# Second attention of a four-layer kernel: heads in slots of four, scores on four row groups, part of the softmax shift on GpSimd

## The reference, cut to what matters

```python
q = (x @ wq.T)...; k = (x @ wk.T)...; v = (x @ wv.T)...      # 32 heads of 8
scores = einsum('bhqd,bhkd->bhqk', q, k) / sqrt(8) + rel_bias
ctx = einsum('bhqk,bhkd->bhqd', softmax(scores), v)
x3 = layernorm(x2 + ctx @ wo.T)
```

## Time and profile before

| | |
|---|---|
| median of 3 runs | 955.1 us |
| profiled execution, its own time | 953.87 us |
| its span, first to last instruction | 951.8 us |
| mean granted TensorE clock | 0.978 |
| second attention, eight iterations | about 364 to 735 us, some 46.3 us each |
| busy TensorE, VectorE, ScalarE, GpSimd in one iteration | 44.7, 40.4, 44.0, 6.8 us |

### The profile page before, as it was taken

One profiled execution on the slowest core, in us unless ns is written; L12 is line 12 of the kernel. 1 busy time (PEld: TensorE's weight loads), 2 busy tenths in 40 slices (PEclk: granted clock), 3 DMA queues, 4 the chain that ended last, 5 costly groups with the idle time before them and its releaser, 6 DMA issues.

```text
span 951.8 us, 20997 instructions
## 1 busy us (share of the span) xinstructions
PE 866.0 (91%) x7200; PEld 711.0 (75%) x7200; DVE 702.3 (74%) x2130; ACT 687.0 (72%) x1538; POOL 261.3 (27%) x360
## 2 busy tenths in 40 slices
PE   3777899999999998999999999999998998999994
PEld 2556778788888887676777776767666987899994
DVE  6888878878875557888888989898987462365447
ACT  2778857768676337999999999999998322366646
POOL 0345542322343120200202021111112256334432
PEclk8889999999999999999999999999999999999998
DMA  6203021110010012010202020202021212244534
GB/s 200 67 1 98 15 79 62 40 35 13 13 45 13 24 34 61 21 28 1 70 2 70 1 70 2 69 1 59 10 66 48 86 62 94 73 109 124 133 136 174
DMA packets 54760, 54.85 MB, mean 58 GB/s; under 512 B 17953, under 2 KB 48929, under 8 KB 54658
## 3 DMA queue, kind: packets, MB, share of 16 engines
q1 hardware_dynamic: 51250, 44.18, 16.0%
q0 software_dynamic: 3408, 9.34, 2.8%
HBM read 32.85 MB, written 20.65 MB: 56 GB/s over the span
## 4 chain that ended last, share of the span: by engine, by line
PE 50%; DVE 19%; ACT 18%; issue 8%; DMA 2%; POOL 1%; another core or an unknown queue 1%; DVEq 0%; ACTq 0%; SPq 0%; POOLq 0%
PE ps L445 11%; PE ps L447 9%; PE ps L446 9%; PE ps L969 5%; ACT G L1492 4%; ACT G L1502 4%; ACT wu_rows L1492 3%; PE ps L986 3%; PE ps L957 2%; PE ps L677 2%; PE ps L692 2%; DVE G L2037 2%; ACT RT L1252 1%; PE ps L750 1%; DVE wu_rows L2037 1%
## 5 line engine op out<-in xcount | busy, mean ns | idle before, releaser
L1492 ACT ACTIVATE G<-G,small 128x256 f32<-128x256 f32 x296 | 133.7, 517 | 7.0 <-DVE small L2037 7.0
L445 PE MATMUL ps<-WU 128*128 128x256 f32 x384 | 117.4, 306 | 17.3 <-DVE wu_rows L1859 6.7
L2037 DVE CUSTOM_DVE_ANT_0 G<-ps,nb 128x256 f32<-128x256 f32 x296 | 111.6, 419 | 20.7 <-PE ps L957 17.8
L1502 ACT COPY G<-ps 128x512 f32<-128x512 f32 x192 | 113.3, 590 | 9.6 <-PE ps L969 9.5
L2398 POOL TENSOR_SCALAR_AFFINE_SELECT G<-G 128x256 f32<-128x256 f32 x128 | 76.3, 619 | 145.8 <-ACT G L1337 145.6
L446 PE MATMUL ps<-WU 128*128 128x256 f32 x384 | 108.7, 283 | 0.0
L447 PE MATMUL ps<-WU 128*128 128x256 f32 x384 | 108.6, 283 | 0.0
L1492 ACT ACTIVATE wu_rows<-wu_rows,small 128x256 f32<-128x256 f32 x216 | 98.1, 518 | 3.2 <-DVE small L2037 3.2
L969 PE MATMUL ps<-ident,G 128*128 128x128 f32 x592 | 92.6, 283 | 4.6 <-ACT G L1502 3.3
L2037 DVE CUSTOM_DVE_ANT_0 wu_rows<-ps,nb 128x256 f32<-128x256 f32 x216 | 81.6, 419 | 14.6 <-PE ps L957 13.4
L445 PEld LDWEIGHTS ps<-WU 128*128 128x128 f32 x384 | 73.1, 190 | 25.8 <-DVE WU L1865 9.5
(11 more groups left out here) (251 smaller groups left out, 2354.5 us busy)
## 6 DMA issues: line engine op xcount, KB each, us to landing
xs<-G SPq DMA_DIRECT2D x8, 645.0 KB, 6.5
G<-xs SPq DMA_DIRECT2D x39, 128.0 KB
G<-x SPq DMA_DIRECT2D x17, 256.0 KB, 3.4
G<-in_x SPq DMA_DIRECT2D x16, 256.0 KB, 2.8
wu_rows<-yy SPq DMA_DIRECT2D x8, 512.0 KB, 7.6
x<-G SPq DMA_DIRECT2D x15, 256.0 KB, 2.4
wu_rows<-in_wu SPq DMA_DIRECT2D x8, 384.0 KB, 5.7
wraw<-in_wu SPq DMA_DIRECT2D x8, 256.0 KB, 2.9
```

The source lines that it names most:

```text
L445: pe.matmul(o, lh, rh, start=start, stop=False, skip_group_check=True)
L1492: m = act.activation(p, p, ACT.Exp, scale=-1.0, bias=mneg[:, k:k + 1])
L1502: act.copy(probT(h), halves(2 + h % 2)).then_inc(probT_act, 1)
L2037: m = dve.tensor_tensor_reduce(prob(H2 * i + h)[:, t, :], ps[:, SCORE_BANKS[(H2 * i + h) % 3], S * t:S * (t + 1)], nbv[:, t, :], 1.0, -FMI ...
```

## The change

Heads are done in slots of four (`QUADS`, eight per iteration). `scores(i, q)` issues four heads into four banks, `SCORE_BANKS = (0, 1, 5, 6)`, and waits until all four heads of the slot before have been read. Turns of a quad are in the slot after; a mix covers eight heads, in slots 1, 3, 5 and 7, between scores and turns. Bank 6 is no longer there for the neighbours' work: it goes to bank 4, shared with the mixes (`SHARED_BANK`), and bank 7 (`DENSE_BANK`). For 12 heads of 32 the exponential moves behind the transpose: GpSimd subtracts the minimum in `prob`, TensorE turns the result, and ScalarE takes it with an exponential of 128x512 out of PSUM instead of a copy. ScalarE takes all heads. GpSimd's weight splits are laid between its subtractions.

```diff
+QUADS = H2 // 4
+SCORE_BANKS = (0, 1, 5, 6)
+SHARED_BANK, DENSE_BANK = 4, 7
+POOL_SHIFTS = (1, 2, 2, 1, 2, 1, 2, 1)
@@ banks of the neighbours' work
+        def b_qk(f, b, t):
...
+                return (DENSE_BANK if t else SHARED_BANK) if b else 6
@@ TensorE, scores
+                    if i or q:
+                        pe.wait_ge(biased_ready, 4 * (QUADS * i + q))
...
                     for t in range(2):
+                        for j in range(4):
                             r = slice(32 * j, 32 * j + 32)
+                            m = pe.matmul(ps[:, SCORE_BANKS[j], S * t:S * (t + 1)], QT[r, q, P * t:P * (t + 1)], KTT[r, q, :],
                                           start=True, stop=True, tile_position=(32 * j, 0))
+                    m.then_inc(score_ready[2], 1)
@@ TensorE, turn
+                    if j < POOL_SHIFTS[quad % QUADS]:
+                        pe.wait_ge(prob_shifted, shifts(n))
+                    else:
+                        pe.wait_ge(prob_ready, n + 1 - shifts(n))
+                    if n >= 2:
+                        pe.wait_ge(probT_taken, n - 1)
@@ TensorE, one iteration
+                    for q in range(QUADS):
+                        scores(i, q)
+                        if q == 1 and not first:
+                            pe.wait_ge(heads_k[2], 4 * i + 3)
+                            mix(i - 1, 3)
+                        if q == 3:
+                            if left:
+                                pe.wait_ge(v_staged[2], i + 2)
+                            mix(i, 0)
+                        if q == 5:
+                            if left:
+                                pe.wait_ge(split_hi[2], 8 * (i + 1) + 4)
+                                pe.wait_ge(split_ready[2], 4 * (i + 1) + 2)
+                            pe.wait_ge(o_copied[2], 4 * i + 1)
+                            mix(i, 1)
+                        if q == 7:
...
+                            mix(i, 2)
+                        before = H2 * i + 4 * q - 4
+                        if before >= 0:
+                            turn(before)
+                            turn(before + 1)
...
+                        if q == 5 and left:
...
+                            qk(2, i + 1, 1)
+                        if q == 6 and left:
+                            pe.wait_ge(split_ready[2], 4 * (i + 1) + 4)
+                            turned(QS, DENSE_BANK, 0)
+                            pe.wait_ge(o_copied[2], 4 * i + 2)
+                            turned(KS, SHARED_BANK, 0)
...
+                        if before >= 0:
+                            turn(before + 2)
+                            turn(before + 3)
+                        if q == 0 and left:
+                            heads_out(2, i, 2)
+                            pe.wait_ge(heads_q[2], 4 * i + 3)
+                            x_turn(2, i + 1)
...
+                        if q == 4 and left:
...
+                            qk(2, i + 1, 0)
@@ ScalarE
+                    if n % 4 < POOL_SHIFTS[n // 4 % QUADS]:
+                        act.activation(probT(n), halves(2 + n % 2), ACT.Exp, scale=-1.0).then_inc(probT_taken, 1)
+                    else:
+                        act.copy(probT(n), halves(2 + n % 2)).then_inc(probT_taken, 1)
...
+                    for q in range(QUADS):
+                        before = H2 * i + 4 * q - 4
+                        if before >= 0:
+                            take(before)
+                            take(before + 1)
...
+                        if before >= 0:
+                            take(before + 2)
+                            take(before + 3)
+                        if q == 4 and not first:
+                            context_hi(2, i - 1)
...
+                        for j in range(POOL_SHIFTS[q], 4):
+                            exponential(H2 * i + 4 * q + j)
+                        if q in (4, 5) and left:
+                            hi_parts(i + 1, q - 4)
@@ VectorE: least of the four heads first, take gone, then
+                        if q == 4:
+                            if not first:
+                                context_lo(2, i - 1)
+                            if left:
+                                qk_lo_parts(i + 1, 0)
+                        if q == 5:
+                            outputs(i, 1, first)
+                            if left:
+                                qk_lo_parts(i + 1, 1)
@@ GpSimd
+            def shifted(n):
+                pool.wait_ge(biased_ready, n + 1)
+                for t in range(2):
+                    k = 2 * (n % 8) + t
+                    p = prob(n)[:, t, :]
+                    m = pool.tensor_scalar(p, p, mneg[:, k:k + 1], None, ALU.subtract)
+                m.then_inc(prob_shifted, 1)
...
+                for q in range(QUADS):
+                    if q == 7 and i:
+                        layernorm_rstd(2, i - 1, 2)
+                    for j in range(POOL_SHIFTS[q]):
+                        shifted(H2 * i + 4 * q + j)
+                    if q == 0 and i < iterations[2] - 1:
+                        expert_part(i, 0)
+                    if q == 3:
+                        shared_part(i)
+                    if q == 5 and i < iterations[2] - 1:
+                        expert_part(i, 1)
```

More of the change, by code:

```diff
@@ L406, in raw_count, with shifts @@
             return 16 * sum(dmas(n) for n in range(load + 1))
[L408 to L422, removed]
+        def shifts(n):
+            quad, j = divmod(n, 4)
+            return (sum(POOL_SHIFTS) * (quad // QUADS) + sum(POOL_SHIFTS[:quad % QUADS])
+                    + min(j + 1, POOL_SHIFTS[quad % QUADS]))
         blk = ctx.enter_context(nc.Block())
@@ L668, in heads @@
             def heads(f, b, n):
-                for src, bank, out in ((QS, B_QT[f], heads_q[f]), (KS, B_KT[f], heads_k[f])):
+                for src, bank, out in ((QS, B_QT[f], heads_q[f]), (KS, b_kt(b, n) if f == 2 else B_KT0, heads_k[f])):
                     w = src.bitcast(F32).rearrange("p (t g c) -> p t g c", t=2, g=8)
@@ L944, in phase2, with turned @@
                 n = iterations[2]
[L946 to L952, removed]
+                def turned(src, bank, group):
+                    w = src.bitcast(F32).rearrange("p (t g c) -> p t g c", t=2, g=8)
+                    for g in range(2):
+                        for t in range(2):
+                            m = pe.transpose(ps[:, bank, S * g + P * t:S * g + P * (t + 1)], w[:, t, 2 * group + g, :], ident[:])
+                    m.then_inc(heads_turned[2], 1)
@@ L976, in mix @@
                         pe.wait_ge(vp_ready[2], i + 1)
[L977 to L988, removed]
+                    pe.wait_ge(probT_taken, H2 * i + 8 * g + 8)
@@ new lines, in mix @@
+                    for quad in (2 * g, 2 * g + 1):
+                        for kt in range(2):
+                            for j in range(4):
+                                h = 4 * quad + j
+                                at = (D2 + 1) * h
+                                m = pe.matmul(ps[32 * j:32 * j + 32, SHARED_BANK, S * (quad % 2):S * (quad % 2 + 1)],
+                                              vp[:, kt, at:at + 32], probT(h)[:, kt, :], start=kt == 0, stop=kt == 1,
+                                              skip_group_check=True, tile_position=(0, 32 * j))
@@ new lines, in one @@
+                        if q == 1:
+                            pe.wait_ge(heads_q[2], 4 * i + 4)
+                            turned(KS, DENSE_BANK, 3)
+                        if q == 2 and not first:
+                            c_turn(2, i - 1, 1, 8)
+                        if q == 3 and not first:
+                            c_turn(2, i - 1, 3, 8)
+                        if q == 4 and left:
+                            pe.wait_ge(heads_q[2], 4 * i + 4)
+                            pe.wait_ge(heads_k[2], 4 * i + 4)
+                            pe.wait_ge(o_copied[2], 4 * i + 1)
+                            qk(2, i + 1, 0)
@@ L1031, in phase2 @@
+                        if q == 6 and not first:
+                            if left:
+                                pe.wait_ge(heads_q[2], 4 * (i + 1) + 1)
+                            project(2, i - 1)
+                        if q == 7 and left:
+                            pe.wait_ge(heads_q[2], 4 * (i + 1) + 2)
+                            turned(KS, DENSE_BANK, 1)
                 passes(n, one)
                 pe.wait_ge(out_step[2], OUT_STEPS[2] * (n - 2) + 5)
+                pe.wait_ge(biased_ready, H2 * n)
@@ L1038, in phase2 @@
                     m.then_inc(xt_turned[3], 1)
-                for h in range(H2 - TURN_LAG, H2):
-                    turn(n - 1, h, False)
-                    if h == H2 - 3:
-                        mix(n - 1, H2 // 4 - 2, False)
-                mix(n - 1, H2 // 4 - 1, False)
+                for h in range(H2 - 4, H2):
+                    turn(H2 * (n - 1) + h)
+                pe.wait_ge(o_copied[2], 4 * n - 1)
```

(6 more changed lines are left out.)

271 lines of the change are left out of this document (136 added, 135 removed).

## The result

The changed kernel takes 1064.8 us (median of 4 runs, 1057.4 to 1066.0) against 955.3 before, a ratio of 1.114 with a 95% interval of 1.111 to 1.117. It is slower, as forecast, but by 109 us where I had said 48, and outside the range of 935 to 1040. The profiled execution took 1065.39 us, with a span of 1063.6.

The account below looks back on a forecast made before the run. TensorE and ScalarE were taken as nearly full. Work of 37.8 plus waits of 3.8, 4.5, 2.9 and 4.2 gave 53.2 us against 46.3, 6.9 more in seven iterations: 1003 us, range 935 to 1040.

Parts of the forecast that it names:

- waits that come: Step pricing TensorE's new waits per iteration from handoffs and fixed engine orders: 15.4 us counted.
- the three places: TensorE's waits at slot 5's mix, slot 6's first turned q and slot 2's turns: 11.2 us per iteration.
- The first rival: Waits are covered and the busiest engine, ScalarE, sets the period: 919 us, chance 0.17.
- Slot 5: The mix there waits for high and low parts standing behind a take and exponentials: 3.8 us per iteration.
- Slot 6: The first turned q there waits for its low parts after q and k product part 1: 4.5 us.
- The ring: Turns wait for takes standing behind exponentials, in slots 0, 1, 3, 4 and 7: together 4.2 us per iteration.
- Slot 2: Turns of heads GpSimd shifted wait, since GpSimd stands in a weight split awaiting its load: 2.9 us.
- the cast's slope: Price of GpSimd's 128x256 subtraction, taken from casts of 384 and 704 columns: 0.40 us each.
- TensorE's clock falls as well: Rival: idle in slots 5 and 6 brings half clock, 24 us more, 1027 us; chance 0.22.
- TensorE's own work: TensorE's work per iteration without waits, falling from 43.3 to 37.8 us.
- ScalarE's 38.6: ScalarE's work per iteration after the change, down from 43.0 us.
- the 0.60 for such a take: ScalarE's price in us for each of 12 takes with an exponential, set between 0.47 and 0.81.

Follow-up runs that it names:

- e6: Changed kernel with high parts of q and k early and GpSimd subtracting for no head: 984.8 us.
- e3: Changed kernel with GpSimd's expert splits in later slots, high parts earlier, and the first half of the q and k product earlier: 942.4 us.
- e4: Changed kernel with idle TensorE time filled by 34 products of 512 columns per iteration, in slots 2, 5 and 6: 1029.7 us.

## Why the prediction was wrong

**The direction and its reason were right.** The step "waits that come" named the three places, and all three are where TensorE waits. The first rival, that the busiest engine sets the period, describes e6 (984.8), and about a third of its gain of 36 us became real once the orders were mended (e3, 10 us under the kernel before).

One iteration of the kernel after, 61.5 us, can be taken apart by the marks of idle time in TensorE's timeline: they sum to 14.8 us. In e3, which issues the same work at full clock throughout, they sum to 3.7 of 44.0 us, so TensorE's work takes 40.3 us. The rest, 61.5 - 14.8 - 40.3 = 6.4 us, is my estimate of what half clock costs. The forecast had 15.4 of waits, 37.8 of work and 0 for the clock.

**The waits: right in sum, by luck.** Slot 5: 3.8 forecast, 3.55 in the trace. Slot 6: 4.5 forecast, 0.50 + 3.47. The ring: 4.2 forecast; the trace has 1.07 in slot 4 where I had 1.75, and 0.34 and 0.64 elsewhere, 2.05 in all. Slot 2: 2.9 forecast, 4.55 + 0.69 = 5.2 in the trace. The last two errors, of 2.2 and 2.3 us, cancelled. In slot 2 two terms were mis-sized. The subtraction was 0.91 to 0.93 us, not 0.40, one head 1.0 longer: I took the cast's slope, and even my upper end, the mask's 0.62, was too low. From the transpose of x to the split were 6.2 us (559.51 to 565.71), not 5.3.

**The step that failed is the clock**: "TensorE's clock falls as well" was set apart as a rival with a chance of 0.22, and the sum has the forecast's own time at full clock. Nothing but the waits that I forecast was needed for it: my text had TensorE idle for about 4 us in slots 5 and 6 and cited a stretch with 1.76 of 3.40 us busy that was followed by half clock. I called that stretch "elsewhere"; at 366.90 to 373.70 us it is the start of this same stage. The rival should have been part of the forecast. It was also priced too low, 3.4 us per iteration for two stretches of 3.4: the trace has three places and 17.0 us, because slot 2 has its own and two of the three last 6.8. TensorE is busy for 13.7 us of these, which at half clock lose up to 6.9; the estimate above is 6.4, some 45 us in seven iterations. e4 shows 6.9 us in one iteration and 35 us for the whole kernel, net of what the filling costs.

**The second term is TensorE's own work**: 37.8 forecast, 40.3 by the estimate, 2.5 more, some 17 us in seven iterations. I had counted 43.3 of work and 3 of waits in an iteration before; the marks of idle time there sum to 1.6, which leaves 44.7. And the change took off 4.4 (44.7 to 40.3), not 5.5. Summed from start to start, with the marked waits taken off, an iteration before and one of e3 have:

| us per iteration | before | e3 | forecast |
|---|---|---|---|
| transposes, switches behind them included | 23.7 | 22.7 | 21.6 |
| scores | 6.9 | 3.7 | 3.4 |
| mixes | 8.1 | 7.4 | 7.6 |
| dense products | 6.0 | 6.4 | 5.4 |

The forecast's column is made of the prediction's terms, with its 3 us of switches less the 1.6 removed put to the transposes; it comes to 38.0, since the prediction's 43.3 is 0.2 under its own terms. So the scores, at 0.43 to 0.45 for four heads, and the mixes were priced fairly. Short were the transposes, where fewer switches saved 1.0 us and not 1.6, and the dense products, priced from one weight load to the next. ScalarE's 38.6 came out as 38.3 in e3's window, though not by the terms: two takes with an exponential last 1.09 us, two copies 1.07 to 1.08, so the 0.60 for such a take was too much. That the first iterations are longer (66.1 and 62.6 us between transposes of x, then 61.25 to 61.9) I did not forecast and have not explained.

The Trainium skill (TensorE: Matmul & The Clock Gate, Part 3) gives less than fourfold for four row groups; no run here isolates it, and by the prediction's estimate it would have moved the sum by 4 us.

## What to carry to other kernels

Where an instruction order is written out by hand, read each engine's list between a producer and its last consumer before adding up busy times: here three waits and the clock's falls behind them cost some 120 us, and moving three steps on GpSimd, two on ScalarE and one each on TensorE and VectorE, with no work removed, turned a loss of 109 us into a gain of 10. In the iteration shown each wait of TensorE of 3.4 us or more had two prices, the wait and the slow stretch behind it; a forecast that contains the first should have the second in its sum. And work that may stall on a load doesn't belong on a queue whose next instruction feeds the bounding engine.

## What the runs showed of the hardware that I had not expected

GpSimd's `tensor_scalar` on 128x256 float32 takes 0.85 us (maximum with a number) and 0.93 (subtraction of a column of scalars), while a cast of 384 columns takes 0.50 and an affine select of 256 takes 0.62: per column, one-input instructions differ by more than a factor of two (3.3 against 1.3 ns).

TensorE at half clock did no harm to the other engines' rows: VectorE's low parts take 1.42 us at 591.76 (full clock) and at 604.31 (half clock). In the iteration shown each of the three places where TensorE had little to do was followed by 3.4 or 6.8 us of half clock; filling the waits with 34 otherwise useless products of 512 columns per iteration made the kernel 35 us faster (e4). It doesn't take a wait of 4 us, either. In e6 the longest wait around the fall shown here is 1.75 us (in slot 6, for an exponential):

```profile
546.50:549.90 3.40, 1.88 (x19) 1.38 (x17) 1.85 (x6) 3.06 (x9) 0.00 (x0) 1.00 0.03 7
551.30:554.70 3.40, 3.40 (x18) 3.40 (x17) 1.92 (x9) 2.97 (x7) 0.00 (x0) 0.50 0.00 0
```

An exponential of 128x512 out of PSUM costs ScalarE no more than a copy of it (two take 1.09 us, two copies 1.07 to 1.08), while two exponentials of 256 in SBUF cost 0.81 us between starts, a copy of 512 only 0.47.
